# Making the second attention's rows inside the first feed-forward loop, with the inverse root on VectorE

## The reference

```python
h = _L0_tok_ref(x, ...)                      # wavelets, gated bands
h = jnp.concatenate([h, txt], axis=1)
h = h + _L0_attn_ref(_layernorm(h), ...)     # attention by squared distance
h = h + _L0_ffn_ref(_layernorm(h), ...)      # router, 8 experts of width 128 and a shared one
h = h + _L1_attn_ref(_layernorm(h), ...)     # grouped attention, 16 heads, per image
h = h + _L1_ffn_ref(_layernorm(h), ...)      # router, 8 experts, shared of width 256

def _layernorm(x, axis=-1, eps=1e-05):
    m = jnp.mean(x, axis=axis, keepdims=True)
    v = jnp.var(x, axis=axis, keepdims=True)
    return (x - m) / jnp.sqrt(v + eps)
```

## Time and profile before

| | us |
|---|---|
| median of 3 runs (lowest, highest) | 814.78 (813.91, 816.97) |
| the profiled execution: its time | 820.07 |
| its span, first to last instruction | 818.2 |
| mean granted TensorE clock, share of full | 0.981 |
| PE / PEld / DVE / ACT / POOL busy | 745.6 / 610.5 / 583.7 / 338.8 / 127.3 |

### The profile page before, as it was taken

How to read it: one execution, slowest core, us unless ns; L and a number is a source line. 1 busy time by engine, 2 the same in 40 slices (tenths; PEclk the granted TensorE clock), 3 DMA queues, 4 the chain that set the end, 5 groups by cost and what they waited for, 6 DMA issues and landing times.

```text
span 818.2 us, 13681 instructions
## 1 busy us (share of the span) xinstructions
PE 745.6 (91%) x4993; PEld 610.5 (75%) x4993; DVE 583.7 (71%) x1229; ACT 338.8 (41%) x595; POOL 127.3 (16%) x121
## 2 busy tenths in 40 slices
PE   3279996799999999999999999999998999999997
PEld 3259994699999999865444444444766999999997
DVE  6986767677777777847666666667786677777776
ACT  1214554433333333214777767665433333333332
POOL 0205651000000000070121542222500000000000
PEclk9999996999999999989999999999999999999999
DMA  8500000000000000082345664212200000000000
GB/s 322 208 1 1 0 2 0 1 1 1 1 2 2 0 0 0 2 194 70 81 102 77 118 112 98 41 20 78 127 0 1 1 20 21 1 21 19 2 20 20
DMA packets 21186, 36.54 MB, mean 45 GB/s; under 512 B 6301, under 2 KB 16957, under 8 KB 20489
## 3 DMA queue, kind: packets, MB, share of 16 engines
q1 hardware_dynamic: 16328, 33.12, 15.2%
q10 hardware_dynamic: 4800, 2.66, 2.0%
HBM read 25.79 MB, written 9.95 MB: 44 GB/s over the span
## 4 chain that ended last, share of the span: by engine, by line
PE 83%; DVE 11%; issue 2%; ACT 2%; DMA 2%; POOL 0%; SPq 0%; DVEq 0%; POOLq 0%
PE PS L1248 17%; PE PS L1250 17%; PE PS L1249 17%; PE PS L1507 7%; PE PS L1482 5%; PE PS L1491 5%; PE PS L1515 3%; PE PS L1256 2%; PE PS L1598 2%; DVE MX L1160 2%; PE PS L1331 1%; PE PS L1365 1%; PE PS L1276 1%; DMA x_in<-in_x 1%; PE PS L1565 1%
## 5 line engine op out<-in xcount | busy, mean ns | idle before, releaser
L1160 DVE TENSOR_REDUCE MX<-PS 128x2 f32<-128x576 f32 x144 | 108.7, 756 | 61.8 <-PE PS L1491 61.4
L1086 DVE SCALAR_TENSOR_TENSOR h<-PS,cmb,h 128x256 f32<-128x256 f32 (+1 forms) x342 | 143.9, 476 | 0.2 <-PE PS L1250 0.2
L692 ACT ACTIVATE PR<-PS 96x768 f32<-96x768 f32 x144 | 115.9, 807 | 55.7 <-PE PS L1482 55.2
L633 ACT ACTIVATE sg<-PS 128x384 f32<-128x384 f32 x114 | 56.1, 493 | 164.4 <-PE PS L1250 164.4
L1071 DVE TENSOR_TENSOR al<-aa,ah 128x384 fp32r<-128x384 f32 x114 | 63.6, 558 | 67.1 <-ACT ah L637 67.1
L637 ACT ACTIVATE ah<-aa 128x384 fp32r<-128x384 f32 x114 | 60.0, 526 | 84.0 <-DVE aa L1065 84.0
L1065 DVE TENSOR_TENSOR aa<-sg,PS 128x384 f32<-128x384 f32 x114 | 63.2, 554 | 25.7 <-ACT sg L633 25.2
L1248 PE MATMUL PS<-xTh,W1h 128*128 128x384 f32 x240 | 81.1, 338 | 0.0
L1249 PE MATMUL PS<-xTh,W1l 128*128 128x384 f32 x240 | 80.9, 337 | 0.0
L1250 PE MATMUL PS<-xTl,W1h 128*128 128x384 f32 x240 | 80.8, 337 | 0.0
L1248 PE MATMUL PS<-xTh,W0h 128*128 (+1 forms) x216 | 72.9, 338 | 0.0
(11 more groups left out here) (239 smaller groups left out, 1581.1 us busy)
## 6 DMA issues: line engine op xcount, KB each, us to landing
QS<-scrH SPq DMA_DIRECT2D x28, 144.0 KB, 4.3
W1raw<-in_w SPq DMA_DIRECT2D x1, 3840.0 KB, 12.2
W0raw<-in_w SPq DMA_DIRECT2D x1, 3456.0 KB, 11.3
scrH<-qh SPq DMA_DIRECT2D x8, 432.0 KB, 2.5
scrL<-ql SPq DMA_DIRECT2D x8, 432.0 KB, 2.9
wD<-in_wD SPq DMA_DIRECT2D x1, 2304.0 KB, 11.7
out_tokens<-h SPq DMA_DIRECT2D x6, 384.0 KB, 2.3
x_in<-in_x SPq DMA_DIRECT2D x2, 1024.0 KB, 6.2
```

Of the source, the lines that this page charges most:

```text
L692: A_(PR[0:KT, ca:cb + 1:cb - ca, :], PS[0:KT, b:b + 2, 0:CW], ACT.Exp).then_inc(s["e_exp"], 1)
L1086: ins = V.scalar_tensor_tensor(out=hj, in0=PS[:, b + t // 2, (t % 2) * D:(t % 2) * D + D], scalar=cmb[:, ds(g * GT + t, 1), e:e + 1].squee ...
L1160: V.tensor_reduce(MX[:, hf, z:z + NSH // 2 + 1:NSH // 2], PS[:, b:b + 2, 0:POS], AX_X, ALU.max).then_inc(s["e_mx"], 1)
```

## The change

Rows of groups 0 to 4 are made inside the first FFN's loop, during the experts of the group that follows. `next_rows(g, q)` on VectorE puts, per expert q of nine: statistics of the three tiles (q = 0, 1), sums and the start value of the inverse root by an integer shift (q = 2), two Newton steps (q = 3), a third (q = 4), the normalised tiles (q = 4, 5, 6), copies of the transposed tiles from PSUM into `xT` (q = 5, 6, 7) and their low parts (q = 7, 8). At q = 1 to 8 it stands between `low` and `accumulate`, at q = 0 behind `accumulate`. TensorE transposes a tile at q = 5, 6, 7 between `gate_up` and `down`, and ScalarE writes its high part at q = 6, 7, 8 behind `ah`. The last group is done behind the loop in the old way, with the same root. `W1raw` is loaded in two halves and GpSimd makes all six low slices. `WARM` goes from 8 to 10, `WARM_E` from five counts to two (28, 9), and `busy_at` gives 2 unused matmuls in the first turn's even slots below 11, where it gave 1.

```diff
 REST = NT - GT
-NPW = 4
+NPW = 6
 NE = 8
...
         sp.wait_ge(s["e_rb"], 16 * 2 * HPG * (IMGS - NLATE))
-        sp.dma_start(W_raw[1][:, :], A["w1"]).then_inc(s["d_w1"], 16)
+        half = sum(WCOLS[1]) // 2
+        for n in range(2):
+            sp.dma_start(W_raw[1][:, n * half:(n + 1) * half], A["w1"][:, n * half:(n + 1) * half]).then_inc(s[f"d_w1{n}"], 16)
         with sp.Fori(0, NG) as g:
...
         pool.wait_ge(s["e_const"], 4)
-        pool.wait_ge(s["e_xn"], NG)
+        pool.wait_ge(s["e_xt"], GT * (NG - 1))
+        pool.wait_ge(s["e_xn"], 1)
         def divide(i):
...
                 A_(sc[:, :, :], sc[:, :, :], ACT.Sigmoid).then_inc(s["f1_sig"], 1)
+        def tile_high(g, t):
+            j = g * GT + t
+            act.wait_ge(s["e_xc"], j + 1)
+            A_(xTh[:, :, ds(j * P, P)], xT[:, t], ACT.Copy).then_inc(s["e_th"], 1)
         def experts(L, gu):
             ne = 9 + L
-            def body(r):
+            def body(r, first=False):
                 for k in range(gu * ne):
...
                     A_(ah[:, b], aa[:, b], ACT.Copy).then_inc(s[f"f{L}_ah"], 1)
+                    q = (k - 1) % ne
+                    if L == 0 and not (first and k <= ne) and HIGH_Q <= q < HIGH_Q + GT:
+                        tile_high(r * gu + (k - 1) // ne - 1, q - HIGH_Q)
             turns = NG // gu
-            body(0)
+            body(0, True)
             with act.Fori(1, turns) as r:
...
         experts(0, 2)
-        std(0, REST)
-        prep("e", 0)
+        tile_high(NG - 2, 2)
+        act.wait_ge(s["e_T"], 1)
+        A_(xTh[:, :, REST * P:].rearrange("p k (t c) -> p t k c", t=GT), group_ps(0).rearrange("p t (k c) -> p t k c", k=KC), ACT.Copy).then_inc(s["e_hi"], 1)
         def ring_free(G, ring, a):
...
         A_(unit[:, :], unit[:, :], ACT.Sqrt)
-        act.wait_ge(s["d_w1"], 16)
         for c in range(NG):
+            if c % (NG // 2) == 0:
+                act.wait_ge(s[f"d_w1{c // (NG // 2)}"], 16)
             z = slice(c * n1, c * n1 + n1)
...
                 V.tensor_tensor(al[:, b], aa[:, b], ah[:, b].bitcast(F32), ALU.subtract).then_inc(s[f"f{L}_al"], 1)
-            def tile_stats(n, g, t):
-                dve.wait_ge(s["f0_acc"], n + 1 - t)
-                bn(g * GT + t, h[:, ds(g * GT + t, 1), :].squeeze(1)).then_inc(s["f0_st"], 1)
             def accumulate(n, g, e, k):
...
                     g = r * gu + (k - 1) // ne
+                    q = (k - 1) % ne
+                    ahead_of = L == 0 and not (first and k <= ne)
+                    if ahead_of and q:
+                        next_rows(g - 1, q, n, (k - 1) % 2)
                     if not first or k >= 1:
-                        accumulate(n - 1, g, (k - 1) % ne, (k - 1) % per)
-                    if L == 0 and (k - 1) % ne < GT and (not first or k >= 1 + ne):
-                        tile_stats(n - 2, g - 1, (k - 1) % ne)
+                        accumulate(n - 1, g, q, (k - 1) % per)
+                    if ahead_of and not q:
+                        next_rows(g - 1, 0)
             assert per % 2 == 0
             body(0, True)
-            with dve.Fori(1, NG // gu) as r:
-                body(r)
+            if L == 0:
+                own.loop(1, NG // gu, ROW_OPS * gu, body)
+            else:
+                with dve.Fori(1, NG // gu) as r:
+                    body(r)
             if before_last is not None:
...
         prep("c", xnc, 2)
-        def before_last():
-            dve.wait_ge(s["f0_st"], REST)
-            moments(0, REST)
-            ahead("e", xn1)
-        experts(0, 2, before_last)
+        def tile_bn(g, t):
+            own(V.bn_stats(gst[:, t], h[:, ds(g * GT + t, 1), :].squeeze(1)))
+        def row_sums():
+            own(V.tensor_tensor(gm[:, 0], gst[:, :, 1], gst[:, :, 4], ALU.add))
+            own(V.tensor_tensor(gm[:, 1], gst[:, :, 1], gst[:, :, 4], ALU.subtract))
+            own(V.tensor_tensor(gm[:, 2], gst[:, :, 2], gst[:, :, 5], ALU.add))
+        def row_roots():
+            own.settle()
+            own(V.tensor_scalar(gm[:, 3], gm[:, 0], 0.5, None, ALU.mult))
+            own(V.scalar_tensor_tensor(out=gm[:, 4], in0=gm[:, 1], scalar=0.25, in1=gm[:, 1], op0=ALU.mult, op1=ALU.mult))
+            own.settle()
+            own(V.scalar_tensor_tensor(out=gm[:, 5], in0=gm[:, 2], scalar=1.0 / D, in1=gm[:, 4], op0=ALU.mult, op1=ALU.add))
+            own.settle()
+            own(V.tensor_scalar(gm[:, 0], gm[:, 5], LN_EPS, None, ALU.add))
+            own.settle()
+            own(V.tensor_scalar(gbits[:, 0], gm[:, 0].bitcast(I32), 1, None, ALU.logical_shift_right))
+            own.settle()
+            own(V.tensor_scalar(grs[:, :].bitcast(I32), gbits[:, 0], -1, 0x5f3759df, ALU.mult, ALU.add))
+            own.settle()
+        def newton():
+            own(V.scalar_tensor_tensor(out=gm[:, 1], in0=grs[:, :], scalar=-0.5, in1=grs[:, :], op0=ALU.mult, op1=ALU.mult))
+            own.settle()
+            own(V.tensor_tensor(gm[:, 2], gm[:, 1], gm[:, 0], ALU.mult))
+            own.settle()
+            own(V.scalar_tensor_tensor(out=grs[:, :], in0=gm[:, 2], scalar=1.5, in1=grs[:, :], op0=ALU.add, op1=ALU.mult))
+            own.settle()
+        def tile_rows(dst, g, t):
+            return V.tensor_scalar(dst[:, 0, t], h[:, ds(g * GT + t, 1), :].squeeze(1), gm[:, 3, t:t + 1], grs[:, t:t + 1], ALU.subtract, ALU.mult)
+        def tile_copy(g, t, n, b):
+            dve.wait_ge(s["f0_dn"], n)
+            V.tensor_copy(xT[:, t], PS[:, 5 + 2 * b, D:2 * D].rearrange("p (k c) -> p k c", k=KC)).then_inc(s["e_xc"], 1)
+        def tile_low(g, t):
+            j = g * GT + t
+            dve.wait_ge(s["e_th"], j + 1)
+            V.tensor_tensor(xTl[:, :, ds(j * P, P)], xT[:, t], xTh[:, :, ds(j * P, P)].bitcast(F32), ALU.subtract).then_inc(s["e_tl"], 1)
+        def next_rows(g, q, n=None, b=None):
+            if q == 0:
+                tile_bn(g, 0)
+                tile_bn(g, 1)
+            if q == 1:
+                tile_bn(g, 2)
+                own.settle()
+                row_sums()
+            if q == 2:
+                row_roots()
+            if q == 3:
+                newton()
+                newton()
+            if q == 4:
+                newton()
+            if q in (4, 5, 6):
+                tile_rows(xnc, g, q - 4).then_inc(s["e_xt"], 1)
+            if q in (5, 6, 7):
+                tile_copy(g, q - 5, n, b)
+            if q in (7, 8):
+                tile_low(g, q - 7)
+            if q == 8:
+                tile_low(g, 2)
+        experts(0, 2, lambda: next_rows(NG - 2, 8))
         for t in range(GT):
-            own(bn(REST + t, h[:, REST + t, :]))
+            tile_bn(NG - 1, t)
         own.settle()
-        moments(REST, GT)
-        prep("e", xn1, 0)
+        row_sums()
+        row_roots()
+        for _ in range(3):
+            newton()
+        for t in range(GT):
+            ins = tile_rows(xn1, NG - 1, t)
+        ins.then_inc(s["e_xn"], 1)
+        dve.wait_ge(s["e_hi"], 1)
+        V.tensor_tensor(xTl[:, :, REST * P:].rearrange("p k (t c) -> p t k c", t=GT), group_ps(0).rearrange("p t (k c) -> p t k c", k=KC),
+                        xTh[:, :, REST * P:].rearrange("p k (t c) -> p t k c", t=GT).bitcast(F32), ALU.subtract).then_inc(s["e_lo"], 1)
         def query_rows(i, m):
...
                 M(PS[:, 4, 0:GW], a1h[:, 0, 0:P], a1h[:, 1, :], start=True, stop=True)
-        def rows_for_images():
+        def last_rows():
             pe.wait_ge(s["e_a1h"], 1)
             pe.wait_ge(s["f0_acc"], NG * 9 - 1)
-            keep_warm(12)
-            for g in range(NG):
-                if g > 1:
-                    pe.wait_ge(s["e_lo"], g - 1)
-                transpose_group("e", g, xn1[:, g % 2], g % 2 * 2)
-                if g:
-                    keep_warm(WARM_E[g - 1])
+            keep_warm(WARM_E[0])
+            pe.wait_ge(s["e_xn"], 1)
+            for t in range(GT):
+                for k in range(KC):
+                    at_ = (t % 2) * D + k * P
+                    ins = nc.tensor.transpose(PS[:, t // 2, at_:at_ + P], xn1[:, 0, t, k * P:k * P + P], ident[:, :])
+            ins.then_inc(s["e_T"], 1)
+            keep_warm(WARM_E[1])
+        def tile_transposes(g, t, n, b):
+            wait(pe, s["f0_acc"], n - 1)
+            pe.wait_ge(s["e_xt"], g * GT + t + 1)
+            for k in range(KC):
+                nc.tensor.transpose(PS[:, 5 + 2 * b, D + k * P:D + k * P + P], xnc[:, 0, t, k * P:k * P + P], ident[:, :])
         def experts(L, gu):
...
                         M(PS[:, 7, 0:2 * NE], ones[:, :], tot[:, :], start=True, stop=True).then_inc(s["f1_sum"], 1)
+                    q = (k - 1) % ne
+                    if L == 0 and not (first and k <= ne) and q in (5, 6, 7):
+                        tile_transposes(r * gu + (k - 1) // ne - 1, q - 5, n - 1, (k - 1) % 2)
                     if not first or k >= 1:
...
         experts(0, 2)
-        rows_for_images()
+        last_rows()
```

(27 more changed lines are left out.)

## The result

| us | before | changed |
|---|---|---|
| median of 4 runs each | 815.01 (813.91 to 816.97) | 832.96 (832.73 to 843.42) |
| profiled execution, its time | 820.07 | 832.86 |
| its span | 818.2 | 831.1 |
| mean granted TensorE clock | 0.981 | 0.987 |

The changed kernel takes 1.023 times as long (95% interval 1.018 to 1.028), and 1.023 again in a later set of runs (1.018 to 1.028; 834.1 median). The forecast was 828.4, in a range of 820 to 838. So the sign and the range held, and the rise of 18 us was forecast as 13.6.

A forecast was written before the change was run, and what follows sets the result against it. VectorE's queue order was taken to bound the first FFN's loop, with 0.34 us of room per step. Loop +20.4, behind it -6.8, first turn and weights 0: +13.6 on the 814.78 median, 828.4 us, range 820 to 838.

The forecast's parts named there:

- What bounds a step: First FFN loop: VectorE's late pace is 2.80 of 3.14 us, leaving 0.34 per step; the 0.59 wait can't be filled.
- the work fits into the gaps: Rival, chance 0.08: VectorE's idle time in the loop takes the new work, only 3.0 us of transposes is paid; 810.0 us.
- The loop's sum: First FFN, step 10 to the last `al` at step 53: 155.6 us against 135.2, a loss of 20.4 us.
- the rival on the loop's waits: Chance 0.10: small VectorE operations cost more in the loop, 0.10 behind each of 15 waits per group, 7.5 us; 836.
- The transposes: TensorE's 30 in the loop, 3.0 us in all, cost nothing while TensorE waits for `al`, 3.0 without that cover.
- Behind the loop: From the last `al` to the second attention's first projection: 11.9 us instead of 18.7, a gain of 6.8 us.
- The first turn: Second attention: added warm-up and unused matmuls fill the wait for keys; taken as 0, ends -2.5 and +1.6 us.
- Late weights: VectorE loses 2.9 us of low slices to GpSimd, ahead of the roots; cost taken as 0, between -0.5 and 0.
- The base: +13.6 us on the profiled 820.07 makes 833.7; from the median of the runs, 814.78, it makes 828.4.
- TensorE's clock in the loop: Rival, chance 0.12: pauses drop the clock to half for 6.6 us once per group, 14 us in all; 842.

The follow-up runs named there:

- experiment 3: The changed kernel with the inverse root's moments, start value and Newton steps left out for groups 0 to 4: 819.0 us median, 1.002 of the kernel before.
- experiments 1 and 5: First: changed kernel with VectorE's new work at q = 1 to 8 moved between `gated` and `low`, 818.2 us median; second: the fitted kernel, 814.0 us.
- experiment 4: The changed kernel with TensorE's transposes left out of the loop for groups 1 to 4, waits and copies kept: 834.5 us median, loop 158.5 us.
- the fitted kernel: Changed kernel with new work between `gated` and `low`, a low part, a statistic and a copy reordered, VectorE's turns written out: 814.0 us median, 0.997 of before.
- experiment 2: The changed kernel with VectorE's two loop turns of the first FFN written out, nothing else: 830.6 us median, loop 154.5 us.
- experiment 6: The fitted kernel with `WARM` back at 8 and the first turn's unused matmuls as before the change: 816.0 us median, 0.996 of the kernel before.
- experiment 7: The kernel before with only `WARM` = 10 and the first turn's extra unused matmuls: 816.2 us median, 1.001 of the kernel before.
- the repeat under experiment 8: Second set of the kernel before with only the late weights' edit (two W1raw DMAs, six GpSimd low slices): 820.1 us median, ratio 1.001; profiled execution 829.2 us.

## Why the prediction held, and what it missed

- **What bounds a step** held, and by the mechanism that was named. VectorE's pace of 2.80 us comes back in the loop wherever it is late with nothing new to do (experiment 3), and each 0.1 us beyond 0.34 is paid. The 0.59 us ahead of `al` stayed whole in the changed kernel, as said. TensorE's idle time came as 13 us and not some 20, and more of it for the first normalised tile of a group (7.8 us) than for `al` (4.1): these rows weren't ready a step earlier. The rival "the work fits into the gaps" fell for the order that was given, and its own arithmetic was sound for another: moved into that gap (experiments 1 and 5) the work costs what the transposes cost.
- **The loop's sum** was 155.6 us and came to 157.3; +20.4 was forecast and +22.0 measured. It hides two misses. The operations were dearer in the forecast by 1.1 us (written out, the loop took 154.5): copies, low parts and normalised tiles all cost 0.33, where the sum had 0.40, 0.35 and 0.34. And the loop itself cost 2.8 us that the sum had at nothing: 1.7 in the two steps at the jump, 0.1 at the entry, 0.12 behind each of two root chains in four groups, which makes 1.0. So the rival on the loop's waits has a true part, 1.0 us for its 7.5, and the jump was not thought of. In the kernel before VectorE passes the jump with 0.2 us of delay inside its room.
- **The transposes** were rightly taken at nothing while VectorE is late (experiment 4) and at 3.0 without that cover: the loop of the fitted kernel is 3.2 longer than before. No run leaves them out there.
- **Behind the loop** -6.8 was forecast and -6.6 measured, 12.1 us from `al` to the projection for 11.9. That the unused matmuls cost nothing holds for full clock. With the clock at 0.82 to 0.84 from 350 to 360 us (experiment 2) the last nine took 3.07 us instead of 1.84, and the projection came 0.7 us behind the last low part instead of 0.25; `aa` to projection was 14.7 us there.
- **The first turn** was taken at 0 with ends of -2.5 and +1.6. Both trades in it exist: +1.2 us in a run at full clock, and -2.6 and more where the old turn's clock falls (234.5 us before, 231.9 in experiment 6). How they weigh in a median depends on how many runs fall: alone on the kernel before the new turn moved it by 0.3 us (experiment 7).
- **Late weights**: nothing, as said, though GpSimd starts when the last image's sums are done and not with the first slice.
- **The base.** For the profiled pair +13.6 was forecast and +12.8 measured, and that is closer than the terms are: 1.6 and 0.2 too little in the loop and behind it were made good by 2.5 us ahead of step 10 and in the first turn, most of it clock, which is luck. For the medians the sum was 4.4 us short. Of these, 1.6 is the loop, some 0.2 the stretch behind, and 1.2 the first turn if the runs behind the median of before were at full clock there. The remaining 1.4 may be the clock behind the out projection: 238.6 to 238.7 us from there to the end in the eight profiled executions in which it fell, before and changed among them, and 237.0 to 237.1 in the six in which it stayed full. Whether the runs behind the medians differ in this way isn't shown, and in the later set the two medians are 14.9 apart (834.1 and 819.3), not 18.
- **TensorE's clock in the loop** stayed at 1.00 in the changed kernel and its repeat, with pauses of up to 1.6 us. So the rival had no part in the result: it wanted a fall in every group. It isn't void, though. In experiment 4, whose loop on TensorE differs by the transposes alone, the clock fell once, to 0.50 behind a pause of 1.8 us, and cost 1.2 us. The Trainium skill ("TensorE: Matmul & The Clock Gate", "A second HAM failure mode: psum-queue depth-cycling") says that frequent short pauses make the clock swing: 13 us of pauses in 185 us didn't in the changed kernel, and did once in a loop with about as many.

## What to carry to other kernels

Idle time of an engine is no room until one has seen where in its queue it lies: compare its period when it is late (here 2.80 us) with that of the pipeline (3.14), and only the difference takes more work. A wait for the other engine's part of one's own work (here ScalarE's `ah` between `aa` and `al`) is room too, but only for work put between the two instructions, short enough, and not waiting for that same engine. Of a filler for TensorE's clock ask whether it fills a wait or only stands beside one: the first kept the clock in ten of twelve runs for 1.0 us, the second cost 0.2 us and kept nothing. And before an engine's loop body is made longer, look at the jump: written out, or short as in experiment 3, it cost nothing.

## What the runs showed of the hardware that was not expected

- VectorE stood for 1.37 us with nothing to wait for at the jump back of a `Fori` loop of two groups, and the step over it took 4.9 and 5.0 us in two executions against 3.45 for its like. Written out, it was gone, and with 15 small operations per group less in the body (experiment 3) it was gone as well, with the loop in place and VectorE late. A packet of the instruction queue, 8 KB, stands in that step in each of the four executions that waited there and in none of the others.
- The inverse root from an integer shift and three Newton steps on 3 columns is nearly all latency: each operation is 0.16 us long and starts 0.20 behind the one it waits for, and the 15 in a row behind the loop took 2.85 us (352.43 to 355.28).
- One kernel's runs on one core lay between 813.3 and 833.9 us. With the wait of 0.9 us for the keys filled, ten of twelve lay within 3.3 us. In a long one (the repeat under experiment 8) that wait was 1.38 us, the clock stayed at 0.50 from 360 to 400 us, and projection to out projection took 246.1 us, where 231.9 is the shortest here.
